# Gate products made in the projection stage and stored as tables, in a gated delta-rule layer

## The reference, cut to what matters

```
q = silu(conv(x @ Wq)); k = silu(conv(x @ Wk)) * 128**-0.5; v = silu(conv(x @ Wv))
a = sigmoid(x @ Wa + ba)          # per head and channel: decay
beta = sigmoid(x @ Wb + bb)       # per head
def step(St, inp):                # scan over the 512 steps
    err = einsum('bhvk,bhk->bhv', St, k_t) - v_t
    St = a_t[..., None] * St - (b_t[..., None] * err)[..., None] * k_t[:, :, None, :]
    o_t = einsum('bhvk,bhk->bhv', St, q_t)
```

## Time and profile before

| | us |
|---|---|
| median of 3 runs | 2785.17 (2784.39 to 2795.73) |
| the profiled execution: its time, its span | 2792.46, 2790.7 |
| projections, from the span's start to the last store's landing | 0 to about 931 |
| recurrence | about 932 to about 2020 |
| attention_out, ternary, feed_forward | about 2020 to 2790 |

### The profile page before, as it was taken

The page is one execution under the profiler, slowest core; times in us unless marked ns, Lnnn a source line. Parts: engine busy times, 40 slices in busy tenths (PEclk is TensorE's granted clock), DMA queues, the critical chain, the costliest instruction groups (busy, mean ns, idle before and its releaser), DMA issues. The chain is left out here.

```text
span 2790.7 us, 50619 instructions
## 1 busy us (share of the span) xinstructions
PE 2578.7 (92%) x17812; PEld 2216.3 (79%) x17922; DVE 2042.4 (73%) x5887; ACT 1204.5 (43%) x2393; POOL 1445.2 (52%) x1216
## 2 busy tenths in 40 slices
PE   8999999999999489999999999999749997899999
PEld 6888888888888378888888888888637776788887
DVE  4776778678769279999999999989768886433333
ACT  4445445544454233333333333323568874433333
POOL 2644553455355489999889898979422220000000
PEclk9999999999999799999999999989859999999999
DMA  5466555655664855555556566555654543100000
GB/s 132 129 177 185 150 146 163 187 143 146 171 179 124 266 201 215 200 198 198 215 227 231 214 230 227 214 197 198 240 202 158 213 188 122 67 12 11 11 11 15
DMA packets 417321, 454.39 MB, mean 163 GB/s; under 512 B 122497, under 2 KB 367233, under 8 KB 393857
## 3 DMA queue, kind: packets, MB, share of 16 engines
q1 hardware_dynamic: 417152, 452.22, 48.6%
HBM read 321.49 MB, written 131.14 MB: 162 GB/s over the span
## 5 line engine op out<-in xcount | busy, mean ns | idle before, releaser
L355 PE MATMUL pa_ps<-pa_x_hi,pa_w_hi 128*128 128x512 f32 x1296 | 507.0, 391 | 9.4 <-ACT pa_y L298 5.2
L355 PE MATMUL pa_ps<-pa_x_lo,pa_w_hi 128*128 128x512 f32 x1296 | 505.1, 390 | 0.0
L355 PE MATMUL pa_ps<-pa_x_hi,pa_w_lo 128*128 128x512 f32 x1296 | 504.9, 390 | 0.0
L438 DVE SCALAR_TENSOR_TENSOR pa_cv<-pa_y,pa_taps,pa_cv 128x2048 f32<-128x2048 f32 x144 | 357.1, 2480 | 17.8
L1197 DVE TENSOR_TENSOR pb_tmp<-pb_gb,pb_ps 128x112 f32<-128x112 f32 (+6 forms) x1792 | 328.5, 221 | 25.5 <-POOL pb_gb L787 11.6
L787 POOL TENSOR_TENSOR pb_gb<-pb_gb,pb_ng 128x448 f32<-128x448 f32 (+6 forms) x448 | 331.6, 786 | 2.9 <-DMA pb_gb<-scratch_pairs 2.9
L1202 DVE TENSOR_TENSOR pb_ps<-pb_ps,pb_tmp 128x112 f32<-128x112 f32 (+6 forms) x1792 | 330.8, 226 | 0.0
L355 PEld LDWEIGHTS pa_ps<-pa_x_hi,pa_w_hi 128*128 128x128 f32 x1296 | 243.6, 188 | 67.1 <-ACT pa_y L298 9.4
L771 POOL TENSOR_TENSOR all_res<-all_res,pb_crow 128x1024 f32<-128x1024 f32 x120 | 281.9, 2367 | 6.1 <-DMA pb_crow<-scratch_crow 6.1
L355 PEld LDWEIGHTS pa_ps<-pa_x_hi,pa_w_lo 128*128 128x128 f32 x1296 | 243.7, 188 | 50.7
L355 PEld LDWEIGHTS pa_ps<-pa_x_lo,pa_w_hi 128*128 128x128 f32 x1296 | 243.6, 188 | 50.0
(11 more groups left out here) (191 smaller groups left out, 5426.9 us busy)
## 6 DMA issues: line engine op xcount, KB each, us to landing
pb_crow<-scratch_crow SPq DMA_DIRECT2D x30, 2048.0 KB, 10.0
pb_gb<-scratch_pairs SPq DMA_DIRECT2D x64, 896.0 KB, 6.6
pa_o_ng<-scratch_beta SPq DMA_DIRECT2D x16, 1024.0 KB, 7.9
scratch_ng<-pa_o_ng SPq DMA_DIRECT2D x16, 1024.0 KB, 4.5
scratch_A<-pa_o_A SPq DMA_DIRECT2D x16, 1024.0 KB, 4.5
scratch_vt<-pa_o_vt SPq DMA_DIRECT2D x16, 1024.0 KB, 4.5
scratch_q<-pa_o_q SPq DMA_DIRECT2D x16, 1024.0 KB, 6.9
scratch_g<-pa_o_g SPq DMA_DIRECT2D x16, 1024.0 KB, 7.8
```

The source lines that it names most:

```text
L355: last = nc.tensor.matmul(out, w[:, mat, k, :], xx[:, k, b * S:(b + 1) * S], start=(k == 0 and n == 0), stop=(k == KT - 1 and n == 2))
L438: nc.vector.scalar_tensor_tensor(out=out, in0=yy[:, :, k:k + S], scalar=tap(k), in1=out, op0=ALU.mult, op1=ALU.add).then_inc(s_tap, 1)
```

## The change

`projections` gets three more GpSimd multiplications per head: `vt` by `ng` (2048 elements, after the products of the ratios and before their cumulation), `rg` = `ng` of blocks 1 to 3 by the ratio `r` (1536 elements, written over `ra`), and `cg` = `ng` by the cumulative decay (2048 elements, written over `ng` once the plain `ng` is stored). SyncE stores both new tables, behind `A`. In the `recurrence`, SyncE loads `cg` into `W` and `rg` into a tile, by halves, before `start` needs them; `start` and `cross` multiply by these tables instead of by decays, so that their results are the gated right-hand sides, and the first multiplication of each `solve` and ScalarE's copy `ngx` (L927) go. `w_of` and `x_of` are one region now.

```diff
 # projections
-        N_PR = 21
+        N_PR, N_VT, N_A = 24, 18, 15
@@ SyncE, head
                 if not first:
-                    sp.wait_ge(s_st["ng"], 16 * h)
+                    sp.wait_ge(s_st["cg"], 16 * h)
...
                 sp.wait_ge(s_pr, N_PR * (h + 1))
                 store("A")
+                store("rg")
+                store("cg")
@@ GpSimd, head
                 k = mul(rv[:, 0, :, 1:, 0:1], to(tA, 7)[:, :, :-1, NBL - 1:], to(tI, 0)[:, :, 1:, 0:1])
+                pool.wait_ge(s_ng, h + 1)
+                mul(flat(tI), flat(tI), flat(outs["ng"]), k)
...
-                step(nc.gpsimd.tensor_copy(rv[:, 1, :, :, 0:1], rv[:, 0, :, :, 0:1]))
+                k = step(nc.gpsimd.tensor_copy(rv[:, 1, :, :, 0:1], rv[:, 0, :, :, 0:1]))
+                scale = lambda i: r_out[:, i, :, :, :].rearrange("p c b n -> p (c b) n").unsqueeze(3).broadcast_to([P, NCH * B, NBL, BL])
+                k = mul(by_block(outs["rg"]), by_block(outs["ng"])[:, :, 1:, :], scale(0)[:, :, 1:, :], k)
+                pool.wait_ge(s_st["ng"], 16 * h + 16)
+                mul(by_block(outs["cg"]), by_block(outs["ng"]), scale(1), k)
@@ ScalarE, before exp into ra
+                    act.wait_ge(s_st["rg"], 16 * h)
@@ VectorE, scaled_v
-                dve.wait_ge(s_pr, N_PR * (h + 1))
+                dve.wait_ge(s_pr, N_PR * h + N_VT)
 # recurrence
+            def load_gates(c, hf):
+
+                half = slice(HALF * hf, HALF * (hf + 1))
+                for name, dst in (("cg", W), ("rg", rg)):
+                    src = flat(scr[name][c, :, :, :]).rearrange("p (h t) -> p h t", h=HB)[:, half, :]
+                    sp.dma_start(flat(dst[:, half, :]), flat(src)).then_inc(s_gl[hf], 16)
@@ SyncE, cycle (and both halves of chunk 0 at the stage's start, behind load_rr)
                 if kind != FIRST:
+                    sp.wait_ge(s_wn[1], 6 * c)
+                    load_gates(c, 1)
...
                 sp.wait_ge(s_m, NBL * (c + 1))
-                sp.wait_ge(s_ngx, c + 1)
-                sp.wait_ge(s_sv, scaled(c, 3, 0))
-                sp.wait_ge(s_sv, scaled(c, 1, 1))
                 load(ng[:, :, :], "ng", c + 1, s_ngl)
+                sp.wait_ge(s_wn[0], 6 * (c + 1))
+                load_gates(c + 1, 0)
@@ VectorE, start
-                tt(w_of[hf][:, 8 * q:8 * q + 8, :], src[:, :, 0, 0:BL], rr[p][:, 1, hs, 0:1].broadcast_to([P, 8, BL]), ALU.mult)
-                tt(blocks(W[:, hs, :])[:, :, 1:, :], blocks(src[:, :, 0, :])[:, :, 1:, :], cr[:, :, 1:, :], ALU.mult)
+                tt(x_of[hf][:, 8 * q:8 * q + 8, :], src[:, :, 0, 0:BL], W[:, hs, 0:BL], ALU.mult)
+                tt(W[:, hs, BL:], src[:, :, 0, BL:], W[:, hs, BL:], ALU.mult)
@@ VectorE, solve
-                tt(xs, ws, gates, ALU.mult).then_inc(s_sv, 1)
@@ VectorE, cross
-                    rb = groups(rr[p][:, 0, hs, n + 1:n + 2]).broadcast_to([P, 8, 4, BL])
-                    tt(groups(w_of[hf]), src[:, :, 1, :, :], rb, ALU.mult).then_inc(s_wn[hf], 1)
+                    tt(groups(x_of[hf]), src[:, :, 1, :, :], groups(rg[:, hs, BL * n:BL * (n + 1)]), ALU.mult).then_inc(s_wn[hf], 1)
@@ VectorE, before start of half 1 and of half 0
+                dve.wait_ge(s_gl[1], 32 * (c + 1))
+                    dve.wait_ge(s_gl[0], 32 * (c + 2))
```

More of the change, by code:

```diff
@@ L83, in projections @@
         outs = {n: m.sb(f"o_{n}", [P, NCH, B, CH]) for n in ("q", "k", "ng", "vt", "A", "g")}
+        outs["cg"] = outs["ng"]
+        outs["rg"] = ra[:, :, :].rearrange("p b s -> p (b s)")[:, 0:TOK * (CH - BL) // CH].rearrange("p (c b t) -> p c b t", c=NCH, b=B)
         r_out = m.sb("r_out", [P, 2, NCH, B, NBL])
@@ L118, in projections @@
         s_vt = m.sem("vt")
-        s_st = {n: m.sem(f"st_{n}") for n in ("q", "k", "ng", "vt", "A", "g", "r")}
+        s_st = {n: m.sem(f"st_{n}") for n in ("q", "k", "ng", "vt", "A", "g", "r", "rg", "cg")}
         x_rows = x.rearrange("b (s p) d -> (b s) p d", p=P)
@@ L206, in _ @@
             nc.gpsimd.memset(r_out[:, :, :, :, :], 0.0).then_inc(s_g, 4)
+            flat = lambda t: t[:, :, :, :].rearrange("p c b t -> p (c b t)")
+            by_block = lambda t: t[:, :, :, :].rearrange("p c b (n i) -> p (c b) n i", i=BL)
             at = lambda t, i: t[:, :, :].rearrange("p b (c n i) -> p i b c n", n=NBL, i=BL)[:, i]
@@ L252, in head @@
                 k = mul(rv[:, 0, :, 1:, 0:1], to(tA, 7)[:, :, :-1, NBL - 1:], to(tI, 0)[:, :, 1:, 0:1])
+                pool.wait_ge(s_ng, h + 1)
+                mul(flat(tI), flat(tI), flat(outs["ng"]), k)
+                assert n[0] == N_VT
                 for j in range(1, NBL):
@@ L513, in recurrence @@
         gb = [m.sb(f"gb{i}", [P, HB, PAIRS]) for i in range(NBL)]
-        ngx = m.sb("ngx", [P, HALF, CH // 2])
+        rg = m.sb("rg", [P, HB, CH - BL])
         tmp = m.sb("tmp", [P, HB, BL - 1])
@@ L519, in recurrence @@
         psT, psD, wx = ps[0:2], ps[2:6], ps[6:8]
-        w_of = [t[:, 0:HALF * BL].rearrange("p (h t) -> p h t", t=BL) for t in wx]
-        x_of = [t[:, HALF * BL:2 * HALF * BL].rearrange("p (h t) -> p h t", t=BL) for t in wx]
+        x_of = [t[:, 0:HALF * BL].rearrange("p (h t) -> p h t", t=BL) for t in wx]
         s_id = m.sem("id")
@@ L546, in recurrence @@
         s_sv = m.sem("sv")
-        s_ngx = m.sem("ngx")
+        s_gl = [m.sem(f"gl{i}") for i in range(2)]
         s_rs = [m.sem(f"rs{i}") for i in range(2)]
@@ L586, in recurrence @@
         turn = lambda c, n, hf: 2 * NBL * c + [[0, 2, 3, 5], [4, 6, 7, 9]][hf][n] - 1
-        scaled = lambda c, n, hf: 27 * turn(c, n, hf) + 1
         @block.sync
@@ L697, in _ @@
             load_rr(0, 0)
+            for hf in range(2):
+                load_gates(0, hf)
             sp.dma_start(all_decays, scr["r"][1, :, :, :, :, :].rearrange("c p h b n -> p c (h b n)")).then_inc(s_cr, 16)
@@ L1179, in solve @@
                     dve.wait_ge(s_w, 2 * c + hf + 1)
-                    dve.wait_ge(s_ngl, 16 * (c + 1))
                 else:
                     dve.wait_ge(s_wn[hf], 6 * c + 2 * n)
-                gates = ng[:, HALF * hf:HALF * (hf + 1), BL * n:BL * (n + 1)]
-                if hf and n >= NBL // 2:
-                    dve.wait_ge(s_ngx, c + 1)
-                    gates = ngx[:, :, BL * n - CH // 2:BL * (n + 1) - CH // 2]
-                ws, xs = w_of[hf], x_of[hf]
-                tt(xs, ws, gates, ALU.mult).then_inc(s_sv, 1)
+                xs = x_of[hf]
                 dve.wait_ge(s_m, NBL * c + n + 1)
-                dve.wait_ge(s_sv, 27 * k + 1)
                 quarters = [(q, slice(QUART * q, QUART * (q + 1)), slice(QUART * (2 * hf + q), QUART * (2 * hf + q + 1))) for q in range(2)]
@@ L1199, in solve @@
                     for q, qs, hs in quarters:
-                        dve.wait_ge(s_sv, 27 * k + 1 + 4 * t + q + 1)
+                        dve.wait_ge(s_sv, 26 * k + 4 * t + q + 1)
                         done = s_sv if w > 1 else s_x[hf]
@@ L1261, in _ @@
             dve.wait_ge(s_rl[0], 32)
+            dve.wait_ge(s_gl[0], 32)
             for j in range(4):
@@ L1955, in layer @@
 def layer(nc, x, Wq, Wk, Wv, Wa, ba, Wb, bb, Wg, Wo, cqw, cqb, ckw, ckb, cvw, cvb, ln_w, ln_b, W_up, W_gate, W_down, out):
-    scr = {n: nc.dram_tensor(f"scratch_{n}", (NCH, P, NH, CT), F32, kind="Internal").ap() for n in ("q", "k", "ng", "vt", "A", "g", "o")}
+    scr = {n: nc.dram_tensor(f"scratch_{n}", (NCH, P, NH, CT), F32, kind="Internal").ap() for n in ("q", "k", "ng", "vt", "A", "g", "o", "cg")}
+    scr["rg"] = nc.dram_tensor("scratch_rg", (NCH, P, NH, B * (CH - BL)), F32, kind="Internal").ap()
     scr["beta"] = nc.dram_tensor("scratch_beta", (NH, TOK), F32, kind="Internal").ap()
```

10 lines of the change are left out of this document (3 added, 7 removed).

## The result

The changed kernel takes 2954.07 us (median, 2952.63 to 2959.77), beside 2787.78 for the kernel before (2784.39 to 2795.73): a ratio of 1.060, 95% interval 1.057 to 1.062, so 166 us slower. The forecast was 2996, the range 2870 to 3065.

The account below looks back on a forecast made before the run. It took TensorE and a loop through VectorE, SyncE and beta to bound projections, TensorE the recurrence. Projections +227 us and recurrence -16 gave +211, hence 2996 us against the median; range 2870 to 3065.

Parts of the forecast that it names:

- The lock: Projections: GpSimd instructions reading SBUF block VectorE's two-input SBUF instructions for their whole length; all 11.1 us a head count.
- the longer train: Projections: with rg and cg added, SyncE's queue takes 33.3 us from GpSimd's end to the next gate product.
- the other side: Projections: the new work fits GpSimd's gap, leaving only the recurrence's gain; 2769 us, down to 2722; chance 0.04 for faster.
- The first loop: Projections: gate product (B) through VectorE to weights' issue (W), then queue to next B; 39.0 + 11.1 + 16.2 = 66.3 us.
- The row of 3.04 us: Profile row cited for blocking: a 6-element VectorE copy took 3.04 us beside a long GpSimd instruction.
- beta landing less than 9 us after its issue: Projections: a sign that the prediction fails, if it happened in spite of the longer queue of stores.
- The second loop: Projections: GpSimd's end, store queue, gate product (B), GpSimd's next start; 2T = 137.7, so period T = 69 us a head.
- The constant 6 us of waiting for taps: Projections: GpSimd's three new instructions each first wait for a running VectorE tap; 6 us a head, bounds 2.4 and 7.3.
- Both ends: Projections, outside the 13 steady periods: first to second head 21 us, last but one 15, last head's stores 12.
- The recurrence, -16: Recurrence: 1.2 us a chunk gained, 17 over 14 chunks, some 4 at first and last chunks, less 5 at start.
- TensorE's clock: Projections, rival: TensorE becomes the bound through clock falls, 5 us a head more; 3070 us; chance 0.06.
- The longer stores: Projections: storing rg and cg costs 2.6 and 3.0 us a head; rg at twice cg would be 6 us.

Follow-up runs that it names:

- e1: Changed kernel storing only a sixteenth of rg and cg, with the recurrence's two tables loaded from scratch_ng; 2950.23 us.
- e9: Changed kernel with only the first of its three GpSimd products (vt by ng), stores kept; 2858.66 us.
- e3: Changed kernel with the three GpSimd products replaced by a tiny product and memsets that write without reading, stores kept; 2886.7 us.
- e6: Kernel before the change, with the next head's beta loaded right behind the store of q instead of last of the head; 2780.09 us.
- e5: Kernel before the change in its projections, with the changed kernel's recurrence loading its two tables from scratch_ng; 2779.73 us.
- e2: Changed kernel without its three GpSimd products, storing the same bytes in the same queue places; 2792.22 us.
- e4: Changed kernel with the next head's beta loaded right behind the store of q instead of last of the head; 2933.74 us.
- e8: Changed kernel with the three products moved from GpSimd to VectorE and the next head's beta loaded right behind q's store; 2848.43 us.

## Why the prediction came out as it did

**Direction and order of size: right.** The lock, the longer train and the small gain in the recurrence are all there, and the other side (work in GpSimd's gap) isn't.

**The first loop, 66.3 us: right.** The sum 39.0 + 11.1 + 16.2 is measured by itself in e1 as 49.4 + 16.3 = 65.7; e9 (one product, +4.0) and e3 (memsets, none) confirm the mechanism. The row of 3.04 us was no test of a lock on two-input instructions, since it is a copy with one input; the taps and splits of this kernel and e3's taps are the test. Of the signs named ahead, taps of 5 to 7 us were half right: the products catch weight splits, the first tap and L428 as well. The wait for beta near 11 us and GpSimd's end near +35 are each seen as a pair of values around them. One sign named for failure did appear, beta landing less than 9 us after its issue (583.32 to 591.29, 8.0 us, and 652.58 to 661.08, 8.5): it was badly chosen, since before the change it is 8.1 us too.

**The second loop, T = 69: right in kind, its terms too long.** The long heads have the equation's parts: GpSimd's end at +37.2 (forecast 35.5), the queue behind it 32.6 (33.3), sum 69.8 (68.8). But the heads don't share one period T. The equation runs from a B to GpSimd's next start, through GpSimd's work and the queue to the B after next, so it sets only the sum of two heads; the first loop limits how short one of them can be. With the forecast's own terms that would still be 137.7 us a pair. Measured it is 133.2:

| part of the pair | forecast | measured |
|---|---|---|
| B (527.93) to GpSimd's next start (584.49) | 48.2 + 11.1 = 59.3 | 56.6 |
| GpSimd, start to end (628.47) | 28.0 + 11.1 + 6 = 45.1 | 44.0 |
| queue to the B after next (661.08) | 33.3 | 32.6 |

So the term most off is the first: in the short head the three products lengthen VectorE's part by 7.9 us (46.9 instead of 39.0 from B to W) and not by 11.1. There GpSimd starts 10.8 us ahead of B instead of 6.8, more of its work lies in the 12.9 us in which VectorE idles for beta, and it ends at +26.7. A late B thus makes the head that starts with it short, shorter even than e1's 65.7. The constant 6 us of waiting for taps did little harm, since the pair holds only the long head's GpSimd work. The pair gives 66.6 us a head (66.05 over the 13 periods, seven of which are short).

What the train adds to the lock is the difference to e1: 4.1 us in the long head, less 2.3 in the short, 0.9 a head. I had given it 2.7 (69 less 66.3). That doesn't make the lock the whole cost: without it, but with GpSimd's later end and the longer train, e3 still takes 61.5 us a head on average, 6.3 more than before. The two loops overlap, and either alone makes the kernel slower (e1, e3).

**Both ends: about right**, 44 us measured for 48, in part by luck: the last but one head was 4 over, the first 5 and the last 3 under.

**The recurrence, -16: right in size, misread in part.** The loads of `vt` give 64.4 us a chunk before and 63.1 after, over 14 chunks -18 us (forecast 1.2 a chunk, -17), and the start costs 6.7 (forecast 5). The trace also has 8 us less in the last chunk, 71.1 before and 63.0 after, but that isn't the change's work: e6 runs the same old recurrence with 64.6 there and takes 9.7 us less for the stage than the kernel before. Against e6 the stage gains 13 us. Of the 4 us forecast for the first and last chunks some 1.6 are seen. Long chunks of this kind come and go (e1 has one of 70.5, e5 two); what makes them is open. Without those 9.7 us the 22.5 of the trace and the 11 of e5's medians are close.

VectorE's waits for TensorE grew by 32.8 us, 2.3 a chunk (forecast 3). The forecast read its 0.9 us a chunk from two waits of TensorE's matmuls, and one of them, 6.6 us, is for ScalarE's copy of X and not for VectorE; the other grew (10.8 us, 6.0). TensorE's idle time didn't shrink either: it is busy 860.76 of 900 us, 863.80 before. What did shrink is a wait of its weight loads, which the profile lists apart as PEld, before and after:

```profile
PEld pb_ps L983 <- ACT pb_X L879: 30.0, 51, 1.1
PEld pb_ps L1001 <- ACT pb_X L901: 10.1, 41, 2.8
```

The kernels with the old recurrence have 30.0 and 32.2 us there (e6), those with the new one 10.1 and 7.6 (e2). That is 1.4 us a chunk, about what a chunk gained. The copy of X runs behind VectorE's solve (ScalarE waits 200.1 us for L1202 before), so a shorter solve brings X to TensorE sooner: the forecast's idea, but through ScalarE. ScalarE's deleted copy, which I costed at nothing, may be part of it; no run tells it apart.

**TensorE's clock: right to leave out.** It is granted at 0.50 for 3.5 us after an idle time of 7.65, and 0.93 over the stage, but TensorE waits for others in each head whatever its clock.

**The longer stores.** Cutting `rg` and `cg` to a sixteenth took 3.8 us off the time from GpSimd's end to the next B (32.6 to 28.8), where I had 5.6 for the two, and 0.9 us off the head. The 3.8 is a lower bound of what they cost, since e1's queue waits 4.3 us a head for VectorE: from the store of `A` to the end of that of `q` SyncE takes 13.1 us in the long head and 7.9 in e1. The queue's rate while `rg` and the start of `cg` move in the long head, columns as in rows 1:

```profile
632.00:634.00 2.00, 2.00 (x11) 1.65 (x10) 1.86 (x2) 0.00 (x0) 0.00 (x0) 1.00 1.17 331
634.00:636.00 2.00, 2.00 (x11) 1.65 (x10) 1.86 (x2) 0.00 (x0) 0.00 (x0) 1.00 1.19 318
```

It is 348 GB/s in the 2 us ahead of them, with `A` alone, and 347 in the 2 behind. `A`, `rg` and `cg`, 2816 KB together, move in some 8.5 us, an estimate from these rates; I had 8.6 for the three. By the rule cited ahead from the Trainium skill, "DMA: Bandwidth & Descriptors", section "Specifications", with the prediction's estimate of `rg` at twice `cg`, it would be 12. These rows don't show such a cost for pieces of 384 B.

## What to carry to other kernels

Before moving work to an engine with idle time, look at what that work shares with the bound: here 12.4 us of GpSimd products (as long as in the first head), with 27 us of idle time to hold them, cost VectorE's part of the head 10.4 us, since they read SBUF beside VectorE's two-input instructions; on VectorE itself they cost 6.4. Where a loop runs through a resource of the next round (a tile, a load), solve for the sum over two rounds and limit each round from below by the other loop, and don't take what one engine costs another for a constant: it shrinks in a round in which one of them idles. And when a wait is removed, follow what it had been hiding: in e4 and e8 the engine that had run undisturbed in VectorE's wait became the bound.

## What the runs showed that was not expected

- The same kernel, with the same work in each head, alternates between two periods all through a stage (63.4 and 69.8 us; in e3 54.8 and 68.2). A mean over heads hides it, and a saving in the queue (e1) removes the alternation and little time (0.9 us a head).
- A memset on GpSimd, which reads nothing, leaves two-input taps alone but holds L456, a TENSOR_SCALAR from SBUF: 4.51 us instead of 1.34 beside memsets of 1.60 and 1.81, 2.75 beside one of 1.59. The section of the Trainium skill named above has tensor_scalar among the operations that can enter a mode with two ports and then contend with GpSimd; these rows agree.
- A load moved forward by itself gave 10 us in a kernel whose TensorE was busy 98% of the stage (e6): 811.6 of 830 us had looked like the bound.
